# Second-layer products issued column group by column group instead of row group by row group

## The reference

```python
pos = grid_q[:, :, None, :] - grid_kv[:, None, :, :]
bias = jnp.sign(pos) * jnp.log1p(jnp.abs(pos))
bias = jax.nn.relu(bias @ cpb_w1 + cpb_b1)     # 2 -> 32
bias = jax.nn.relu(bias @ cpb_w2 + cpb_b2)     # 32 -> 32, the "second layer"
bias = (bias @ cpb_w3 + cpb_b3)                # 32 -> 1
sim = jnp.einsum('bhid,bhjd->bhij', qh, kh) + bias
```

## Time and profile before

| what | value |
|---|---|
| median of three runs | 993.13 us |
| the profiled execution, its own time | 995.93 us |
| its span, first to last instruction | 994.1 us |
| TensorE (PE) busy | 858.1 us, 86% of the span |
| TensorE weight loads (PEld) busy | 285.9 us |
| VectorE (DVE) busy | 727.3 us, 73% |
| ScalarE (ACT) busy | 639.7 us, 64% |
| mean granted TensorE clock | 0.948 of full speed |

### The profile page before, as it was taken

One profiled execution on the slowest core, in us unless ns is written; L12 is line 12 of the kernel. 1 busy time (PEld: TensorE's weight loads), 2 busy tenths in 40 slices (PEclk: granted clock), 3 DMA queues, 4 the chain that ended last, 5 costly groups with the idle time before them and its releaser, 6 DMA issues.

```text
span 994.1 us, 33269 instructions
## 1 busy us (share of the span) xinstructions
PE 858.1 (86%) x15332; PEld 285.9 (29%) x15332; DVE 727.3 (73%) x473; ACT 639.7 (64%) x710; POOL 61.5 (6%) x40
## 2 busy tenths in 40 slices
PE   2199997789999998779999998879999999999846
PEld 1133322223333322214233332313323333323212
DVE  3679779697887748697978648967978776797511
ACT  1357677757767655856767765666776685687611
POOL 2200002300000002030000002040000000000000
PEclk8589999899999999889999999979999999999958
DMA  3211010020102001002011001002010200100010
GB/s 136 64 40 46 4 45 4 7 48 9 47 3 71 2 2 46 7 1 55 25 25 52 20 1 46 8 2 51 6 47 10 63 2 24 25 3 2 2 45 21
DMA packets 29530, 27.81 MB, mean 28 GB/s; under 512 B 22096, under 2 KB 24016, under 8 KB 29392
## 3 DMA queue, kind: packets, MB, share of 16 engines
q1 hardware_dynamic: 29392, 25.69, 9.9%
HBM read 23.05 MB, written 2.49 MB: 26 GB/s over the span
## 4 chain that ended last, share of the span: by engine, by line
PE 62%; DVE 22%; ACT 8%; issue 4%; DMA 2%; SPq 0%; POOL 0%; ACTq 0%; DVEq 0%; POOLq 0%
PE pair L790 23%; PE scores L802 18%; DVE h L578 12%; PE pair L785 7%; ACT h L430 3%; PE scores L812 3%; PE pair L940 3%; PE pair L930 2%; PE pair L896 1%; DVE probs L711 1%; PE pair L907 1%; DVE big L681 1%; PE pair L889 1%; DVE neg_max L704 1%; DVE big L675 1%
## 5 line engine op out<-in xcount | busy, mean ns | idle before, releaser
L430 ACT ACTIVATE h<-pair 128x1024 f32<-128x1024 f32 x512 | 496.1, 1021 | 256.8 <-PE pair L790 256.7
L578 DVE TENSOR_TENSOR h<-hx,hy 128x2048 f32<-128x2048 f32 x256 | 580.7, 2315 | 3.2 <-PE pair L790 3.0
L790 PE MATMUL pair<-h,wts 32*32 32x512 f32 x8192 | 345.6, 608 | 55.1 <-DVE h L578 55.1
L802 PE MATMUL scores<-h,wts 128*32 128x512 f32 x2048 | 276.0, 611 | 0.9 <-ACT h L430 0.9
L785 PE MATMUL pair<-fy,u_rows 32*32 32x512 bf16 x4096 | 127.9, 388 | 35.0 <-DMA fy<-fy_dram 20.5
L790 PEld LDWEIGHTS pair<-h,wts 32*32 32x32 f32 x8192 | 120.6, 104 | 84.7 <-DVE h L578 72.2
L785 PEld LDWEIGHTS pair<-fy,u_rows 32*32 32x32 bf16 x4096 | 40.4, 88 | 228.9 <-issue 199.8
L802 PEld LDWEIGHTS scores<-h,wts 128*32 128x32 f32 x2048 | 40.8, 108 | 218.2 <-issue 212.5
L704 DVE TENSOR_REDUCE neg_max<-pair 128x16 f32<-128x1024 f32 x16 | 19.5, 1221 | 61.1 <-PE pair L889 61.1
L310 POOL TENSOR_TENSOR conv_prod<-qpad,wts 128x288 f32<-128x288 f32 x16 | 21.6, 1378 | 475.7 <-ACT qpad L456 475.7
L737 DVE SCALAR_TENSOR_TENSOR x<-pair,wts,x 128x1024 f32<-128x1024 f32 x4 | 5.1, 1283 | 57.0 <-PE pair L940 57.0
(11 more groups left out here) (90 smaller groups left out, 366.7 us busy)
## 6 DMA issues: line engine op xcount, KB each, us to landing
hx<-features_dram SPq DMA_DIRECT2D x64, 128.0 KB, 2.7
hy<-features_dram SPq DMA_DIRECT2D x64, 128.0 KB, 3.1
att_den<-reciprocals_dram SPq DMA_DIRECT2D x4, 512.0 KB
wts<-weights_dram SPq DMA_DIRECT2D x2, 960.0 KB, 8.4
fy_dram<-fy_part SPq DMA_DIRECT2D x96, 8.0 KB, 1.5
x<-x_dram SPq DMA_DIRECT2D x2, 512.0 KB, 5.8
fy<-fy_dram SPq DMA_DIRECT2D x64, 12.0 KB
out_dram<-x SPq DMA_DIRECT2D x2, 512.0 KB, 5.0
```

The source lines that it names most:

```text
L430: emptied("z", 2 * g + j, act.activation(h2[g % H2_BUFS][:, 2 * j:2 * (j + 1)].rearrange("p r n -> p (r n)"), pair_of("z", 2 * g + j)[:], ...
L578: dve.tensor_tensor(h1[g % H1_BUFS][:].rearrange("p c (y x) -> p c y x", x=W), hx[unit % 2][:, :, t].unsqueeze(2).broadcast_to([128, CT, H ...
L790: ins = pe.matmul(z[r][32 * c:32 * (c + 1)], w(l, "w2")[key[r], key[r]], h1[g % H1_BUFS][key[r], c], start=False, stop=True)
L802: ins = pe.matmul(scores[phase % 2][32 * r:32 * (r + 1)], w(l, "w3")[:, 32 * t:32 * (t + 1)], h2[g % H2_BUFS][:, r], start=False, stop=t = ...
```

## The change

The two loops around the float32 products are exchanged: for each column group c the four row groups r are issued in turn. The same 16 products are issued, each into the same place and with the same operands. The semaphore of pair 0 is now incremented by the product (r = 1, c = 3), the 14th of the 16, and that of pair 1 by (r = 3, c = 3), the 16th. Before, it was the 8th and the 16th. The bf16 products ahead of them keep their order.

```diff
                 pe.wait_ge(h1_ready, g + 1)
-                for r in range(ROWS):
-                    for c in range(CT):
+                for c in range(CT):
+                    for r in range(ROWS):
                         ins = pe.matmul(z[r][32 * c:32 * (c + 1)], w(l, "w2")[key[r], key[r]], h1[g % H1_BUFS][key[r], c],
                                         start=False, stop=True)
-                    if r % 2:
-                        filled("z", 2 * g + r // 2, ins)
+                        if c == CT - 1 and r % 2:
+                            filled("z", 2 * g + r // 2, ins)
```

## The result

The changed kernel took 1008.21 us (median of six runs, 1004.06 to 1011.68) against 993.09 us (992.26 to 996.33) of the kernel before: a ratio of 1.0147, 95% interval 1.012 to 1.0173. (The ratios here are worked out from all runs; the quotient of these two medians is 1.0152.) It is slower by 1.5%; the forecast was 1007.5 us. The profiled execution took 1008.25 us.

The account below looks back on a forecast made before the run. The chain of waits, 62% TensorE, was taken to bound the kernel. 79 plain steps x 0.167 = 13.2 us, plus 0.7 for held steps and 0.5 for row-group changes: 993.13 + 14.4 = 1007.5 us; range 991 to 1016.

Parts of the forecast that it names:

- Direct effect on L790: L790's own length in a plain step: the pause stays, 8 tiles and then 8 more, so 0 us.
- plain step: TensorE-only step without waits, from L785 to the next L785, 2.49 us; 79 such steps forecast to lose 0.167 us each.
- price for a change of row group: Each of 12 additional row-group changes in L790 costs 0 to 0.005 us; +0.5 us in the sum.
- step 3: Pair 0's semaphore: pair complete at 262.33 instead of 262.06, so ReLU 0 starts 0.27 us later.
- steps 4 and 5: Next L785's second half is held 0.22 us by ReLU 0; the wait feeds itself, plain step 2.65 to 2.68 us.
- Where it doesn't strike: Steps with a larger margin or bound by VectorE lose nothing; held but otherwise free steps add 0.7 us.
- 68 free steps: Steps without waits ahead of L790, neither plain nor held; their larger margin was to spare them the loss.
- 21 held steps: Steps whose L785 waits for the previous ReLU 0, otherwise free; pair 0 complete 0.05 us later, 0.7 us in all.
- A: Faster: L790's 0.19 us pause comes from the row-group order and interleaving removes it; about 985.5 us; chance 0.12.
- B: No change: in held steps the last four tiles count 0.41 us from the first L785; 996.3 us; chance 0.12.
- the arrival limit: TensorE queue: 64 instructions stand ready behind a waiting one; what follows arrives 0.41 us after the first leaves.
- C: Much slower: each row-group change waits for part of a weight load, 0.05 us at half; over 1100 us; chance 0.08.

Follow-up runs that it names:

- e2: Against the kernel before: row groups interleaved only inside each pair, pair 0's semaphore again on the 8th product; ratio 0.9986 (0.9972 to 1.0001).
- e3: The changed kernel with ReLU 0 shortened to 768 of 1024 columns, the rest left out; ratio to the kernel before 0.9929, median 989.89 us.
- e8: The kernel before, old order, with only pair 0's semaphore moved from the 8th to the 12th product; ratio 1.0085 (1.0062 to 1.0107).
- e5: The kernel before with the 16 bf16 products made 4 of 32 rows by 128 columns, old order; ratio 1.0091 (1.0059 to 1.0122).
- e10: The kernel before with four wide bf16 products and ReLU 0 shortened to 768 of 1024 columns; ratio 0.9822, median 980.02 us.
- e4: The kernel before with ReLU 0 shortened to 768 of 1024 columns, the rest left out; ratio 0.9905, median 987.56 us.
- e6: The kernel before with the float32 products issued ahead of the bf16 ones in all steps; ratio 1.0178 (1.0141 to 1.0216).
- e9: The kernel before, in 185 steps: bf16 and float32 products of row groups 0 and 1, then those of 2 and 3; ratio 1.1086.

## Why the prediction was right, and where its sum was not

**Direct effect on L790: 0.** Right. The plain step still has its late arrivals, and a step that has waited shows 1.15 in both orders. The price for a change of row group was put at 0 to 0.005 us; e2, the 1.34 of e3 and the 1.15 show nothing of it, and the 0.5 us in the sum was not there.

**The start of ReLU 0 (step 3).** The direction was right, the size was not. I put ReLU 0 0.10 to 0.13 after the modelled end of the last matmul of pair 0, as in the earlier trace rows. After the change it starts at 262.70, which is the modelled end of L790 itself (261.27 + 1.43), 0.03 after that of pair 0. This is the mis-sized term: in a step of the changed kernel that is not held ReLU 0 starts 1.57 after L785, against 1.40 before, so the delay is 0.17 and not 0.27, and in the settled loop the gap is some 0.03 and not 0.10 to 0.13.

**The loop (steps 4 and 5).** That the hold feeds itself is confirmed by the constant 2.58, and by e8, where it does not and the steps alternate. From the release at 261.20 the sum is 1.50 to the end of L790, 1.02 of ReLU and 0.06, as put down; with no gap between that end and the ReLU this gives the measured 2.58 where I had 2.65 to 2.68. So a plain step lost 0.09 and not 0.167: 7.2 us and not 13.2.

**Where it doesn't strike.** The 68 free steps with a larger margin lost nothing, as said. Two of my sizes were too small. The 21 held steps lost 0.10 each, not 0.05: the release they wait for now comes 0.28 after L785's start (284.48 - 284.20) and not 0.24. And I wrote that ScalarE's later start costs nothing else. It does: in 16 steps where ScalarE is the late one, L785 is held 0.08 to 0.19 longer, 1.9 us in all. With the 1.7 of the two places where the granted clock was down, these make most of the 4.2 us of the last kind.

**The sum.** +14.4 us was forecast, the spans differ by 12.4 and the medians by 15.1. That the total fits is partly luck: 6 us too much in the plain steps, 5 too little in the others, and of those 5 the 1.7 of the clock stood in no term of mine.

**The rivals.** A and B needed the arrival limit to behave otherwise; the last four tiles 0.41 after the release exclude B, and e3 and e5 exclude A (with all four row groups interleaved and nothing held the pause is still there, and fewer instructions ahead remove it in the old order). e2 alone does not exclude A: its pause still falls on the change from row groups 0 and 1 to 2 and 3. C is excluded by e2. The rule that a weight load overlaps only with matmuls of another row group (the Trainium skill, "TensorE: Matmul & The Clock Gate", section "The mechanism") predicts a gain from interleaving. No run here shows one: e2 is at 0.9986.

**A better version.** None of the variants that compute the whole beat the kernel before. e2 equals it. Under the short ReLU 0 the wide products gain: 0.9822 (e10) against 0.9905 (e4), 0.8%. So something is to be had from e5 if ReLU 0 releases its pair some 0.2 us earlier; how to do that with the whole ReLU was not tried.

## What to carry to other kernels

In this kernel the order of independent products was free inside the group that one semaphore reports, and not across two such groups. Interleaving across two groups finishes both at the end of the block, so look for who waits for the first and with what margin: here 0.05 us against a delay of 0.17. If what that reader releases is needed early in the next round, check whether the group's last member now depends on that release, for then the loss returns in every round.

## What the runs showed that I had not expected

- ReLU 0 does not start at a fixed distance from the second pass of the product that carries the semaphore. From that pass's recorded start it is 0.69 us for the 8th product and 0.74 for the 14th where all 16 tiles start together. In the plain step it is 0.72 for the 8th, and 0.62 for the 12th, 14th and 15th. Ends of matmuls in the profile are modelled; what delays the report when more tiles are busy was not measured.
- In the changed kernel four passes of L790 have begun by 261.30, while the bf16 products of row groups 2 and 3, started at 261.20, still run. In the order, the first four products belong to four row groups, so some product seems to have passed a waiting one. The trace does not name the row group, but the times fit c = 1 of row groups 0 and 1: counted from L785's start, the first eight passes begin at 0.226, 0.230, 0.240, 0.243, 0.380, 0.384, 0.394 and 0.397, each 0.226 after the bf16 product that would be of its own tile.
- The same two steps can run at either level of the clock from one kernel to the next, which moves the time by 1.7 us. With differences of 1% between kernels this has to be read beside the ratio.
- Where the float32 products stand first (e6) or between two groups of bf16 ones (e9), the late arrival costs as much or far more: 1.50 us for the block as before, and 2.12 for L791 alone.
